# A graph attention layer with feed-forward parts: in the edge stage, TensorE does the sums and the maxima piece of step j - 1 ahead of the expansion of step j

## The reference, cut to what matters

```python
q = (x @ Wq + bq).reshape(n, H, D)          # H = 4 heads of D = 64; k and v alike
qi, kj, vj = q[dst], k[src], v[src]
alpha = jnp.sum(qi * kj, axis=-1) / jnp.sqrt(jnp.float32(D))
m = jax.ops.segment_max(alpha, dst, num_segments=n)
ex = jnp.exp(alpha - m[dst])
denom = jax.ops.segment_sum(ex, dst, num_segments=n)
a = ex / (denom[dst] + 1e-16)
out = jax.ops.segment_sum(a[..., None] * vj, dst, num_segments=n)
```

## Time and profile before

| | |
|---|---|
| median of 3 runs | 1348.41 us (1346.89 to 1350.81) |
| profiled execution, first to last instruction (it has no other time) | 1474.8 us, mean granted TensorE clock 0.942 |
| its stages | project to 95 us; edges 95 to 838 us; tail 838 to 1474.8 us |
| first to last `prod` (232 steps) | 95.1 to 815.0 us |
| busy share of the whole span | PE 84%, DVE 72%, POOL 63%, ACT 54% |

### The profile page before, as it was taken

How to read it: one execution, slowest core, us unless ns; L and a number is a source line. 1 busy time by engine, 2 the same in 40 slices (tenths; PEclk the granted TensorE clock), 3 DMA queues, 4 the chain that set the end, 5 groups by cost and what they waited for, 6 DMA issues and landing times. The chain is left out here.

```text
span 1474.8 us, 24100 instructions
## 1 busy us (share of the span) xinstructions
PE 1233.3 (84%) x6835; PEld 952.7 (65%) x6835; DVE 1068.6 (72%) x2557; ACT 802.2 (54%) x2505; POOL 924.8 (63%) x885
## 2 busy tenths in 40 slices
PE   7988676766776777767676889999999999999998
PEld 3444454544444544545454478889798899999998
DVE  7646887777877777877788779886757655556655
ACT  1265857575847575666657555555543344444443
POOL 3366566666666665666664556866766477667765
PEclk9999989899888898888989999999999999999999
DMA  7477766676766666767675120101000000000002
GB/s 229 157 225 211 235 192 193 183 203 184 200 187 196 188 200 179 202 185 204 181 199 145 38 70 29 52 28 42 8 15 22 1 22 15 10 21 15 1 12 77
DMA packets 74087, 175.39 MB, mean 119 GB/s; under 512 B 11516, under 2 KB 36667, under 8 KB 73961
## 3 DMA queue, kind: packets, MB, share of 16 engines
q0 software_dynamic: 37632, 124.28, 30.3%
q1 hardware_dynamic: 34657, 48.25, 9.9%
q10 hardware_dynamic: 1672, 1.33, 0.3%
HBM read 159.91 MB, written 13.91 MB: 118 GB/s over the span
## 5 line engine op out<-in xcount | busy, mean ns | idle before, releaser
L694 POOL DMA_INDIRECT ring<-kv_rows,k_srcI x464 | 465.1, 1002 | 280.8 <-issue 121.5
L764 ACT ACTIVATE ring<-ring 128x64 f32<-128x64 f32 x1800 | 439.8, 337 | 15.0 <-issue 13.4
L1297 POOL TENSOR_TENSOR wm<-k_gf,wm 128x512 fp32r<-128x512 f32 (+2 forms) x224 | 259.6, 1163 | 143.4 <-DVE wm L1798 143.4
L1396 ACT ACTIVATE k_gf<-psF,k_scT 128x512 f32<-128x512 f32 (+2 forms) x224 | 162.3, 725 | 251.9 <-PE psF L1567 237.6
L814 PE MATMUL psA<-ring,oh 128*128 128x260 f32 x912 | 273.4, 428 | 6.6 <-DVE k_acc L1023 5.4
L784 PE MATMUL psQ<-k_q,ohT 128*128 x1392 | 221.1, 300 | 66.7 <-issue 63.3
L1798 DVE CAST wm<-k_gf 128x512 fp32r<-128x512 f32 (+2 forms) x224 | 160.2, 722 | 155.3 <-ACT k_gf L1396 155.3
L989 DVE TENSOR_TENSOR prod<-psQ,ring 128x512 f32<-128x512 f32 x232 | 157.5, 679 | 82.2 <-remote 28.3
L784 PEld LDWEIGHTS psQ<-k_q,ohT 128*128 128x128 bf16 x1392 | 128.8, 103 | 123.0 <-issue 93.9
L814 PEld LDWEIGHTS psA<-ring,oh 128*128 128x128 f32 x912 | 177.3, 216 | 33.8 <-ACT ring L764 6.3
L1029 DVE TENSOR_REDUCE alpha<-prod 128x8 f32<-128x512 f32 x232 | 155.7, 671 | 0.2
(11 more groups left out here) (283 smaller groups left out, 2644.9 us busy)
## 6 DMA issues: line engine op xcount, KB each, us to landing
ohT<-step_destinations SPq DMA_DIRECT2D x29, 512.0 KB
ring<-kv_rows,k_srcI POOLq DMA_INDIRECT x464
kv_rows<-kvst SPq DMA_DIRECT2D x25, 260.0 KB, 2.6
we<-in_L_ffn_W SPq DMA_DIRECT2D x16, 256.0 KB, 2.8
residual<-qst SPq DMA_DIRECT2D x25, 128.0 KB
xs<-in_x SPq DMA_DIRECT2D x2, 1024.0 KB, 9.1
resin<-residual SPq DMA_DIRECT2D x4, 512.0 KB, 4.5
we<-in_L_ffn_Wo SPq DMA_DIRECT2D x8, 256.0 KB, 2.8
```

What stands on the lines that cost most here:

```text
L694: nc.gpsimd.indirect_dma_start(out=ring[:, LT * (j % CP) + k, j // CP:j // CP + 2, :].rearrange("p t e -> p (t e)"), out_offset=None, in_= ...
L764: last = nc.scalar.activation(row[:, 0:D], row[:, 0:D], ACT.Copy, scale=row[:, D:HW_])
L1297: nc.gpsimd.tensor_tensor(low[:, i % 2, m, 0:w], gf[:, n % 4, 0:w], high[:, i % 2, m, 0:w], ALU.subtract).then_inc(s_gl, 1)
L1396: nc.scalar.activation(gf[:, n % 4, 0:cols(g)], ps, ACT.Relu, bias=bias, scale=scale).then_inc(s_ev, 1)
```

## The change

TensorE's order within a step: `rest(j - 1)` now stands ahead of `expand(j)` and of the query projection. No instruction is added or removed, and no other engine's order is touched.

```diff
             def at(i, j, fresh):
 
+                if j > 0:
+                    rest(i, j - 1, fresh)
+                elif not fresh:
+                    rest(i - 1, RING - 1, False)
                 if live(i, j, fresh):
                     expand(i, j, fresh)
                 if fresh and QEARLY + j < NB:
                     project(QEARLY + j)
-                if j > 0:
-                    rest(i, j - 1, fresh)
-                elif not fresh:
-                    rest(i - 1, RING - 1, False)
 
             walk(at)
```

## The result

The changed kernel takes 1492.84 us, the median of 4 runs (1489.95 to 1497.63), beside 1347.65 us before: 145.2 us more, a ratio of 1.1068, interval 1.1046 to 1.109. The forecast was 1492 us. A later comparison, both kernels on one chip, gave 1493.95 beside 1349.1 us, 1.1078 (1.1032 to 1.1124).

What follows compares the result with a forecast made beforehand. VectorE (19.4 us a chunk) and POOL (20.0) were taken as close bounds of the edge stage. 1348.4 + 119 us of stalls + 25 us of low clock = 1492 us; 8 in 10 between 1430 and 1550.

Steps and rivals of the forecast that it cites:

- The chain: Edge stage, from VectorE's result through the waiting piece, register load and expansion to the next prod: 1.75 us.
- Rival A: TensorE's queue: register load and first weight load run ahead of the waiting piece, chain 1.27 us; 1395 us, chance 0.08.
- The stalls: VectorE waiting for the expansion at its next prod, behind pieces of jj 0 to 5: 5.38 us a chunk.
- The base: Edge stage of the unchanged kernel in a timed run: 231 periods in 593.5 us, 20.55 us a chunk.
- The subtraction of 126.4 us: Profiled execution's excess over the median run, taken as standstills of that execution, all in the edge stage's 719.9 us.
- The clock: TensorE in the edge stage: one step in ten to nine at low clock, adding 25 us.
- The sum: Whole kernel: 119 us of stalls and 25 us of clock on 1348.4 us, giving 1492 us.
- POOL: Gathers in the edge stage: 20.0 us a chunk; waits for prod far above 84.7 us, less for L814.
- B: Ring: earlier sums free POOL, up to 40.4 us back if the chain is under about 0.5 us; 1328 us, chance 0.04.
- C: VectorE's existing rests take up the stalls, so no change; needs 5.4 us of rest a chunk; 1348 us, chance 0.04.
- D: TensorE at low clock nearly throughout the edge stage: 276 us more, 1624 us, chance 0.06.

Runs made afterwards that it cites:

- e2_piece_ahead: Kernel before with only the piece of the chain of maxima, not the sums, moved ahead of the expansion: 1584.87 us beside 1476.89 before, ratio 1.0739.
- e1_sums_ahead: Kernel before with only the sums of step j - 1 moved ahead of the expansion, the piece staying behind: 1499.08 us beside 1476.89 before, ratio 1.0133.
- e3_load_ahead: Kernel after with the node block's register load issued ahead of rest(j - 1): 1539.01 us beside 1476.89 before, ratio 1.0425 to the kernel before.
- e4: Kernel before with rest(j - 1) ahead of expand(j) only at jj 3 of each chunk: 1360.15 us beside 1349.1 before, ratio 1.008.
- e5: Kernel before with rest(j - 1) ahead of expand(j) only at jj 0, 6 and 7: 1358.65 us beside 1349.1 before, ratio 1.0062.
- e0_before: Kernel before, unchanged, profiled again: 1479.01 us beside 1476.89 before, ratio 1.001.
- e12_one_gather: Kernel before with one gather a step instead of two from step 32 on, leaving out half the edges' rows: 1333.78 us beside 1479.04, ratio 0.9009.
- e7_two_ahead: Kernel before with each expansion issued one step earlier, expand(j + 1) in place of expand(j): 1370.76 us beside 1349.1 before, ratio 1.0158.

## Why the prediction was right, step by step

- **The chain.** 0.05 + 0.75 + 0.86 + 0.09 = 1.75 us was forecast, and the medians measured at jj 0 to 5 are 1.75 to 1.78. e2_piece_ahead shows that the waiting piece makes it and e1_sums_ahead that the sums don't, e3_load_ahead that 0.55 of its 0.75 us is the register load behind the wait.
- **Rival A** didn't come true: the expansion starts 0.74 us behind the piece (662.97, 663.71). e3_load_ahead says why: a register load stands in between, and only when it is issued ahead of the wait is the expansion close behind. The Trainium skill ("TensorE: Matmul & The Clock Gate", the table of the engine) states that TensorE's queue can pull weight loads ahead of matmuls in flight. No run here shows one go ahead of a matmul that waits: even in e3_load_ahead the expansion's first weight load starts at 646.54, behind the piece at 646.35.
- **The stalls.** 5.38 us a chunk were forecast. VectorE's idle time before prod is 162.0 us in the kernel after, of which 115.1 + 44.3 are the two rows above, against 151 forecast without the clock's share, which was some 11 us (below). jj 2 was 1.40 instead of 1.23: there inh takes 0.41 us, as in 14 of 29 chunks, where it took 0.18 in the chunk that I read.
- **The base.** 20.55 us a chunk and 593.5 us for the periods. The periods of the kernel after take 740 us, and the change cost 145.2 us, which leaves 595 us for before, 20.6 a chunk. From the fourth chunk on e4 and e5 have means of 20.7 and 20.5 us and are 0.39 and 0.34 over before, so there before takes 20.1 to 20.4. The number was good and its reason was wrong. I took the standstills to belong to the profiled execution. They belong to the chip (or the session on it): e0_before's other nine runs took as long as the profiled one. The subtraction of 126.4 us worked, by luck, as the median was that of a chip without them (like 1349.1 us here), and the trace looks like those of the chips with them (e0_before).
- **The clock.** 25 us were forecast, one step in ten to nine at about 1 us each. The count was right: 22 of 232 expansions took over 1.2 us, with a granted clock of 0.92 in the stage. The price was not: from step 24 on, the 19 periods with such an expansion are 11.3 us longer than the medians of their places, 0.6 us each. That is the expansion's 0.6 alone; it leaves nothing for the slow sums, up to 0.8 us in the forecast. So the term is 11 to 13 us. What brings the low clock about isn't shown: TensorE pauses for over 1 us 76 times in this stage, and its clock is low in 16 stretches (112 us).
- **The sum.** 119 + 25 = 144 us forecast, 145.2 measured. The clock's share was too large by some 12 us, and the 119 too small by about as much: they set the 24.8 us of an undisturbed chunk against 20.55, a mean in which the long chunks at the start are contained. Against the 20.1 to 20.4 of the later chunks they come to 123 to 132 us. That the two errors cancel, and the forecast is met within 1 us, is luck; the mechanism is not.
- **POOL.** Here a step of the text failed: POOL was to wait for prod far more than 84.7 us and less for L814. It is the other way, 156.5 us for L814 and 19.8 for prod. Only the first is the change's doing. On the chip without standstills the nearly unchanged e4 and e5 have 17.0 and 18.5 us for prod and 13.4 and 19.0 for L814, so the 84.7 of the earlier trace rows came with the standstills (e3_load_ahead, with them, has 80.5 and 117.5). The sums that free a ring place stand right behind the expansion that prod waits for, and end after 1.04 us, while prod is made after 0.69: once VectorE is the one that is late, the sums come last. It moves no time, as POOL needs 20.0 us of a chunk of 24.8.
- **Rivals B, C and D.** B's condition, a chain under 0.5 us, was not met. C's rest exists and did take up 0.9 us a chunk (e4_only_jj3), a sixth of the stalls. D would have had the low clock nearly throughout; one expansion in ten had it.

What stays open: what the standstills are. They are on two of the three chips of these groups, by their times in every execution of before there, at some 60 places of 1 to 5 us, and not behind step 32 of e12_one_gather. In the earlier trace rows VectorE takes a result of TensorE 3.3 us after its matmul's recorded end. No run takes the DMA traffic away without the instructions, so the cause isn't shown. Nor was the kernel after run on such a chip, so its ratio there is not known; its near kin e2 and e3 are at 1.074 and 1.042. No version here that does all the work beats the kernel before.

## What to carry to other kernels

Before two blocks of an in-order queue change places, look up for each wait in the first what is queued behind it and who needs that next: the price is the time from the wait's release to that engine's need, and it is read from two rows of a timeline. A piece that waits for the current step must stand behind the work that the next step needs, and that work must not wait for this step either (e7_two_ahead). A register load behind a waiting instruction cost 0.55 us here each time; issue it ahead of the wait.

## What the runs showed of the hardware that was not expected

- The same kernel takes 1349.1 us on one chip and 1476.9 and 1479.0 on two others, each within 0.5%. The profiles at the longer time show pauses of VectorE of 1 to 5 us; those over 0.8 us add up to 138 us in the profile of before. A profile and a median from two chips may not be subtracted unless one knows that.
- With half of the gathers (147 GB/s instead of 192 in the stage) the kernel took 1333.78 us on a chip of 1479.04, a gain of 145 us, of which POOL's limit can explain some 20 (an estimate: 20.0 less 19.2 us in 25 chunks). The pauses over 1 us ended with the step at which the gathers were halved.
- TensorE at the low clock behind pauses of 1.14 and 1.39 us between stretches of work: four sum matmuls 1.91 us instead of 1.04. Yet a period with a slow expansion was only 0.6 us longer, which leaves nothing for the slow sums.
